# Layer 1 attention: products with the values of two steps issued together, in the even steps

## The reference

```
def _L1_attn_ref(x, wq, wk, wv, wo):
    B, T, DIM, NH = (2, 512, 512, 16)
    HD = DIM // NH
    ...
    q, k, v = (proj(wq), proj(wk), proj(wv))
    sin, cos = rope_tables(t, HD, dtype=x.dtype)
    q, k = apply_rope(q, k, sin, cos)
    att = jnp.einsum('bhqd,bhkd->bhqk', q, k) * (1.0 / math.sqrt(HD))
    att = jax.nn.softmax(att, axis=-1)
    y = jnp.einsum('bhqk,bhkd->bhqd', att, v)
    y = y.transpose(0, 2, 1, 3).reshape(b, t, c)
    return y @ wo.T
```

## Time and profile before

| | us |
|---|---|
| median of 3 runs | 3033.28 (3030.64 to 3036.55) |
| profiled execution, its own time | 3032.01 |
| its span in the profile | 3030.3 |
| PE busy | 2858.4 (94%) |
| DVE busy | 1869.5 (62%) |
| POOL busy | 1413.5 (47%) |
| ACT busy | 1298.3 (43%) |

### The profile page before, as it was taken

How to read it: one execution, slowest core, us unless ns; L and a number is a source line. 1 busy time by engine, 2 the same in 40 slices (tenths; PEclk the granted TensorE clock), 3 DMA queues, 4 the chain that set the end, 5 groups by cost and what they waited for, 6 DMA issues and landing times. The chain is left out here.

```text
span 3030.3 us, 54363 instructions
## 1 busy us (share of the span) xinstructions
PE 2858.4 (94%) x19392; PEld 2007.7 (66%) x19392; DVE 1869.5 (62%) x2724; ACT 1298.3 (43%) x2021; POOL 1413.5 (47%) x1000
## 2 busy tenths in 40 slices
PE   7999999699999996799999999999999889999999
PEld 5878887578888885455555555555555368888887
DVE  5656767577767764666666666666666754444444
ACT  3221111266666662355555555555555532222222
POOL 2004555022332321377777777777777632222222
PEclk9999999899999998799999999999999999999999
DMA  3211211122222224122222222222222432222221
GB/s 126 88 60 48 69 55 55 32 70 84 85 102 83 83 97 152 56 71 71 71 71 71 70 71 71 71 71 71 71 70 63 139 108 101 84 84 90 87 86 48
DMA packets 124567, 238.99 MB, mean 79 GB/s; under 512 B 13440, under 2 KB 48384, under 8 KB 124416
## 3 DMA queue, kind: packets, MB, share of 16 engines
q1 hardware_dynamic: 120896, 235.32, 23.2%
q10 hardware_dynamic: 3520, 1.46, 0.2%
HBM read 178.02 MB, written 58.72 MB: 78 GB/s over the span
## 5 line engine op out<-in xcount | busy, mean ns | idle before, releaser
L1286 DVE TENSOR_REDUCE l_attn_maxima<-l_attn_ps_max 128x2 f32<-128x1024 f32 x502 | 614.6, 1224 | 239.2 <-PE l_attn_ps_max L1414 227.2
L1257 POOL TENSOR_TENSOR l_attn_summed<-l_attn_summed,l_attn_probs 128x1024 f32<-128x1024 f32 x248 | 587.3, 2400 | 63.5 <-ACT l_attn_probs L1195 63.4
L1195 ACT ACTIVATE l_attn_probs<-l_attn_ps_sc 128x1024 f32<-128x1024 f32 x512 | 497.8, 1029 | 135.0 <-PE l_attn_ps_sc L1402 135.0
L1257 POOL TENSOR_TENSOR l_attn_summed<-l_attn_probs 128x1024 f32<-128x1024 f32 x124 | 293.5, 2389 | 247.5 <-ACT l_attn_probs L1195 247.5
L1661 POOL TENSOR_TENSOR l_ffn_ht_lo<-l_ffn_mixed,l_ffn_ht_hi 128x512 fp32r<-128x512 f32 x88 | 114.0, 1295 | 415.0 <-ACT l_ffn_ht_hi L1682 415.0
L62 PE MATMUL l_attn_ps_prep<-l_w_tile,l_x_tiles 128*128 (+1 forms) x1440 | 285.4, 346 | 10.5 <-DVE l_attn_qk_lo L1280 3.8
L62 PEld LDWEIGHTS l_attn_ps_prep<-l_w_tile,l_x_tiles 128*128 128x128 f32 x1440 | 247.0, 189 | 43.4 <-issue 31.1
L1424 PE MATMUL l_attn_ps_y<-l_attn_probs,l_attn_v 128*32 128x512 f32 x2048 | 272.7, 605 | 1.1 <-ACT l_attn_probs L1195 1.1
L71 PE MATMUL l_ffn_ps_fc<-l_ffn_t_fc,l_ffn_ct_hi 128*128 128x512 f32 x512 | 213.0, 416 | 7.0 <-DVE l_ffn_ct_lo L823 3.6
L71 PE MATMUL l_ffn_ps_out<-l_ffn_t_proj,l_ffn_ht_hi 128*128 128x512 f32 x512 | 205.8, 402 | 0.0
L1138 ACT ACTIVATE l_attn_x_tok<-l_attn_ps_prep 128x256 f32<-128x256 f32 x120 | 46.0, 383 | 372.5 <-DVE l_attn_ps_prep L1275 372.5
(11 more groups left out here) (270 smaller groups left out, 6359.4 us busy)
## 6 DMA issues: line engine op xcount, KB each, us to landing
l_x_tiles<-xt_chunks SPq DMA_DIRECT2D x160, 512.0 KB, 3.8
xt_chunks<-l_ffn_xt SPq DMA_DIRECT2D x32, 512.0 KB, 4.6
l_attn_xin<-in_x SPq DMA_DIRECT2D x32, 256.0 KB, 4.2
l_attn_piece<-in_w_fcT SPq DMA_DIRECT2D x16, 512.0 KB, 4.2
s<-l_attn_s_sb SPq DMA_DIRECT2D x32, 256.0 KB, 2.2
l_attn_piece<-in_w_projT SPq DMA_DIRECT2D x16, 512.0 KB, 3.9
l_ffn_xa<-in_x SPq DMA_DIRECT2D x32, 256.0 KB, 2.6
l_ffn_xb<-in_x SPq DMA_DIRECT2D x32, 256.0 KB, 2.8
```

Source lines behind the costliest of these rows:

```text
L1195: act.activation(probs[kt % RING][:, hs, :], ps_sc[:, hs, :], ACT.Exp, scale=ATT_SCALE).then_inc(exp_done, 1)
L1257: pool.tensor_tensor(total[:, hs, :], old[:, hs, :], probs[kt % RING][:, hs, :], ALU.add).then_inc(added, 1)
L1286: dve.tensor_reduce(maxima[b][:, j, PAIR * hp:PAIR * hp + PAIR, half:half + 1], pair, AX.X, ALU.max).then_inc(max_read, 1)
```

## The change

In even steps PE now issues all four passes of the scores, the first maximum, then the `pv` of **two** earlier steps (s - 2 and s - 1) in a row, the second maximum, and the event. In odd steps it issues no `pv`: three passes, the first maximum, pass 3, the projection, and the second maximum behind the projection. On VectorE `low` of an even step comes right behind that step's two reductions. The prologue and the sharing of additions are not touched, nor is anything on ScalarE, GpSimd or the queues.

```diff
@@ VectorE, tick
                     todo = [(m, parity(p, back), i) for m, back, i in maxes(t, s)]
-                    if todo:
-                        maximum(*todo[0], ps_max[:, :, :])
-                    e = event(t, s - 1) if s else None
-                    if e and e[0] == "turn":
-                        low(e[1], parity(p, EVENTS[s - 1][1]), e[2], ps_prep[:, :, :])
-                    for a in todo[1:]:
+                    for a in todo:
                         maximum(*a, ps_max[:, :, :])
                     e = event(t, s)
                     if e and e[0] == "proj":
                         rope(e[1], e[2], ps_prep[:, :, :])
+                    if e and e[0] == "turn":
+                        low(e[1], parity(p, EVENTS[s][1]), e[2], ps_prep[:, :, :])
@@ TensorE, tick
+                    first = (0, 1, 2) if s % 2 else (0, 1, 2, 3)
                     if live(m, NT):
-                        scores(*mine, (0, 1, 2))
+                        scores(*mine, first)
                     if todo:
                         u, b, i = todo[0]
                         maximum(u, b, i, ps_max, N_MAX * u + i)
-                    if live(m, NT):
+                    if live(m, NT) and s % 2:
                         scores(*mine, (3,))
-                    m, qb, kt = quad(t, s - 1) if s else quad(t - 1, STEPS - 1)
-                    if live(m, NT):
-                        pv(m, parity(p, 0 if s <= CPB else 1), qb, kt)
-                    for u, b, i in todo[1:]:
-                        maximum(u, b, i, ps_max, N_MAX * u + i)
+                    if s % 2 == 0:
+                        for back in (2, 1):
+                            m, qb, kt = quad(t, s - back) if s else quad(t - 1, STEPS - back)
+                            if live(m, NT):
+                                pv(m, parity(p, 0 if s <= CPB else 1), qb, kt)
+                        for u, b, i in todo[1:]:
+                            maximum(u, b, i, ps_max, N_MAX * u + i)
                     if event(t, s):
                         prepare(t, p, s)
+                    if s % 2:
+                        for u, b, i in todo[1:]:
+                            maximum(u, b, i, ps_max, N_MAX * u + i)
```

## The result

| | before | after |
|---|---|---|
| median of 4 runs each, us | 3034.49 (3030.64 to 3036.55) | 3052.89 (3048.16 to 3057.82) |
| ratio, 95% interval | | 1.0063 (1.0048 to 1.0078) |
| profiled execution: own time, span | 3032.01, 3030.3 | 3054.49, 3052.8 |

A forecast was written before the change was run, and what follows sets the result against it. PE was taken to carry the time (192.54 of 200 us busy in the loop). Pairs -4.5, jumps -2, start -1.8, end +5.2 sum to -3.1 us on the profiled 3032.01, median 3030.2, range 3018 to 3044.

The forecast's parts named there:

- The walk through the pair: Loop body, from one second maximum behind a projection to the next: plain pair stays 8.86 us; all pairs together -4.5.
- The start: Step 9 of tick 1: the projection takes the place of the product, -1.8 us.
- the two rules named beside the rows: Skill page: mode changes drain the engine (alone, pair 8.20 us); tiling does not speed up emptying PSUM, which decides the sum.
- the one on PSUM: Loop pairs: emptying PSUM may become the bottleneck; agrees with maxima 1.83 us apart and speaks against the change.
- 8.20: Loop pair in us by PE's own work if the reduction wait did not bind; time 2954, chance 0.02.
- End, tick 16 ... together +5.2: Tick 16, no projection to hide anything: two products in even steps do not fit under ACT's exponentials, +5.2 us.
- tick 17 "at nothing": Tick 17: den costs 0.9 us more, taken as covered by DVE's last additions; without that cover +0.9.
- The slower rival: Loop: DVE and ACT chain to the odd scores longer than PE's; 0.1 us beyond gives 3039, 0.2 gives 3047; chance 0.24.
- The edges of the loop: Six loop jumps: the reduction runs during the jump, -0.3 us each, -2 together, ends -5 and +1.
- if the jump is reached later by the wait in front of the second maximum (up to 1.1 us): Loop jumps, unfavourable case: each would cost 1.7 us in place of 1.5.
- In steps 0 and 8, 0.24 and 0.07 of today's length over a plain turn pair is neither `low` nor DVE, and stays: Loop pairs of steps 0 and 8: this part remains, so they become 9.14 and 8.97 us.

The follow-up runs named there:

- kernel 5: The changed kernel plus eight unread transposes in each odd step without an event at the end (ticks 16, 17); 3040.27 us, 1.0024 of before.
- kernel 6: The kernel before with VectorE's part of the change alone (low right behind its own step's two reductions); 3022.43 us, 0.9961 of before.
- kernel 2: The kernel before with VectorE's order of the changed kernel, and products paired in ticks 16 and 17 only; 3034.60 us, 1.0006 of before.
- kernel 3: The changed kernel with single products and TensorE's old order at the loop's jump (step 15 of odd ticks, step 0 behind); 3043.78 us, 1.0037 of before.
- kernel 7: The changed kernel with VectorE's order of the kernel before, so TensorE's part of the change alone; 3171.18 us, 1.0455 of before.
- kernel 8: The changed kernel with the second maximum before the projection in step 15 of odd ticks, products still paired; 3048.06 us, 1.0051 of before.
- kernel 1: The changed kernel with products paired in ticks 1 to 15 only, single in ticks 16 and 17; 3036.14 us, 1.0019 of before.
- kernel 4: The changed kernel with single products and TensorE's old order both at the loop's jump and in ticks 16 and 17; 3030.20 us, 0.9995 of before.

## Why the prediction was wrong

**Right.** The walk through the pair, each mark within 0.03 us, with its main statement that the wait for the reduction takes what the pairing gives; pairs of step 0 9.16 (predicted 9.14), 4 9.15 (9.19), 8 8.98 (8.97), 12 8.89 (8.90), sum -4.9 for -4.5. The start, -1.7 for -1.8. Of the two rules named beside the rows, the one on PSUM held (the Trainium skill, TensorEngine Tiling (Array Packing), PSUM Bottleneck): the maxima's cadence of 1.83, not the saved drains, set the pair; 8.20 was never seen.

**Wrong: "End, tick 16 ... together +5.2", tick 17 "at nothing".** As a count of TensorE's work it was right (kernel 5: +5.4). It assumed full clock. The term measured +20.2. I had read idle times of 0.54 and 1.14 us per step, and knew that odd steps would lose their product. That this gathers the idle time of two steps in one (1.09 and 0.54 with maxima, 2.12 without), and that the clock might not stay, was not asked. The slower rival was looked for in the loop's chain and not here.

**Wrong: "The edges of the loop", -2, ends -5 and +1.** The text names the right mechanism, "if the jump is reached later by the wait in front of the second maximum (up to 1.1 us)", and prices it at 1.7 for 1.5 per jump. At full clock it was 1.9 for 1.5, near that price; but it was taken as the far end, and -0.3 as the value, though the order has the waiting maximum right in front of the jump. Measured +8.8 for -2: +2.6 by this, and +6.2 by the clock, of which the text has nothing.

**Half right: "In steps 0 and 8, 0.24 and 0.07 of today's length over a plain turn pair is neither `low` nor DVE, and stays".** In kernel 6 it goes (8.90 and 8.87); it stays only under the pairing. Timeline of after, `low` and the projection of a step-0 pair:

```profile
1680.38 0.69 DVE L1280 TENSOR_TENSOR l_wo_lo<-l_attn_ps_prep,l_wo_hi 128x512 fp32r<-128x512 f32 x1
...
1681.38 2.35 PE L62 MATMUL l_attn_ps_prep<-l_w_tile,l_x_tiles 128*128 x12 [0.18 <-issue]
```

In step 0 the projection follows the end of `low` by 0.32 us, in step 8 by 0.13, in steps 4 and 12 by 0.05, in before and after alike. The records of PE's sequencer hold what lies between: two register instructions with waits of their own in step 0, one in step 8, none in step 12. They lengthen the pair where the projection waits for `low`, as it does before the change and under the pairing. In kernel 6 it comes 1.6 us after `low`, and they cost nothing. I costed the VectorE move as a part of the pairing and never alone; taken alone it is the better kernel.

**Open.** The end and the jumps differ between executions: kernels 2, 3, 7, 8 and after are all paired in the end and take 113.5 to 121 us there (of which the marks explain 1.6), and 2 and 6 differ by 17.5 us at the end in the profiles but by 12.2 in the medians. What decides at which of such idle times the clock falls was not settled. Of the 7.8 us that the pairing costs in the loop with the jumps repaired, steps 0, 4 and 8 make some 6 (9.16 for 8.90, 9.15 for 9.11, 8.98 for 8.87, 14 times each), where the projection waits for `low` again, and the jumps 1; the rest was not followed up.

## What to carry to other kernels

Split a change into its parts by engine and cost each alone: here one part was worth -0.4% and the other took more than that away. Where one engine waits for another anyway, batching its work makes one long idle time of two short ones; read the granted clock beside the idle time, and ask whether the batch will then run at half speed in front of something that others wait for. Keep instructions that wait out of the place right in front of a loop's jump.

## What the runs showed of the hardware

- From 2370 to 2430 us the granted clock was 1.00 in before, with idle times of 0.54 to 1.22 us in nearly every step. It was 0.78 in after, with 1.09 and 0.54 us close behind each other in every second step, and later 2.12 us every 8 us. PE was recorded as busy for 45.87 of 60 us in before and 47.60 in after, but the matmuls at half speed are in that second number (372 matmuls, before 474). The Trainium skill (TensorE: Matmul & The Clock Gate, HAM oscillation) tells of such a fall and return at waits for transfers; here the waits are for ScalarE's exponentials and VectorE's reductions.
- One idle time of 2.1 to 2.7 us in a loop otherwise 95 to 96% busy was followed by a fall at three of the six jumps of after, two of kernel 1 and four of kernel 5. With 1.1 to 1.7 us at the same place it was at none, in before and kernels 2, 3, 4, 6 and 8. That is no limit: in the loop of kernel 7, where PE waits 1.7 to 2.0 us in each turn pair, the clock also fell 19 times away from the jumps.
- Eight transposes of 1.09 us per odd step, without use, made the end 14.8 us shorter.
- The loop's jump holds PE's instruction stream for 3.3 to 3.9 us; it costs as much as isn't covered by matmuls issued before it. The jumps of the kernel's shorter loops take 0.21 to 0.25.
